# Adaptive norm, two Mamba passes and a gated FFN: products of u by B of five units moved from GpSimd to TensorE, as products with diagonal matrices

## What is computed

```python
h = layernorm(x) * (1 + ca) + sa
yf = sigmoid(mamba(h, forward weights));  yb = sigmoid(mamba(h reversed, backward weights))
x = x + ga * (layernorm(0.5 * (yf + yb reversed)) * ln_g + ln_b + h)
x = x + gb * ffn(layernorm(x) * (1 + cb) + sb)          # 256 -> 1024 -> 1024 -> 1024 -> 256
# mamba, 512 inner channels, 16 states per channel:
xi = silu(conv4(h @ in_proj));  z = h @ in_proj2
dt, B, C = split(xi @ x_proj, [64, 16, 16]);  dt = softplus(dt @ dt_w + dt_b)
u = dt * xi
for each channel d, state s, token t:   hs[t] = exp(dt[t] * A[d, s]) * hs[t-1] + u[t] * B[t, s]
y[t] = sum over s of hs[t] * C[t, s] + D * xi[t];   out = (y * silu(z)) @ out_proj
```

## Time and profile before

| | us |
|---|---|
| median of 3 runs (lowest, highest) | 4833.41 (4833.06, 4835.86) |
| the profiled execution, its own time | 4838.41 |
| its span, first to last instruction | 4836.5 |
| PE busy | 4305.1 (89%) |
| DVE busy | 3992.5 (83%) |
| POOL busy | 3464.0 (72%), nearly all before 3480 us |
| ACT busy | 3250.3 (67%) |
| granted TensorE clock, mean of the core | 0.965 |

### The profile page before, as it was taken

The page is one execution under the profiler, slowest core; times in us unless marked ns, Lnnn a source line. Parts: engine busy times, 40 slices in busy tenths (PEclk is TensorE's granted clock), DMA queues, the critical chain, the costliest instruction groups (busy, mean ns, idle before and its releaser), DMA issues. The chain is left out here.

```text
span 4836.5 us, 61589 instructions
## 1 busy us (share of the span) xinstructions
PE 4305.1 (89%) x22500; PEld 3149.4 (65%) x22500; DVE 3992.5 (83%) x4222; ACT 3250.3 (67%) x5217; POOL 3464.0 (72%) x1623
## 2 busy tenths in 40 slices
PE   7888888888888888888888888888799999999999
PEld 3565556556555656665555556555678888888888
DVE  6999999999999999999999999999944444444452
ACT  7777777777777777777777777777444444444443
POOL 5999999999999999999999999999820000000000
PEclk9999999999999999999999999999899999999999
DMA  7433333333333333333333333333230111010100
GB/s 264 140 122 124 114 119 114 107 122 112 127 114 116 116 109 118 117 114 118 111 114 111 110 113 114 112 115 127 93 126 31 35 31 36 31 36 31 35 22 9
DMA packets 176850, 475.34 MB, mean 98 GB/s; under 512 B 15073, under 2 KB 99809, under 8 KB 141921
## 3 DMA queue, kind: packets, MB, share of 16 engines
q1 hardware_dynamic: 175648, 459.83, 28.1%
q10 hardware_dynamic: 896, 11.54, 0.7%
HBM read 435.66 MB, written 47.19 MB: 100 GB/s over the span
## 5 line engine op out<-in xcount | busy, mean ns | idle before, releaser
L1293 DVE TENSOR_TENSOR_SCAN m_h<-bank,m_state,m_dBx 128x512 f32<-128x512 f32 x1792 | 2182.1, 1263 | 35.3 <-ACT bank L1059 29.1
L794 PEld LDWEIGHTS bank<-ident,m_h 128*128 128x128 f32 x8192 | 1009.0, 147 | 655.4 <-issue 335.7
L794 PE MATMUL bank<-ident,m_h 128*128 128x128 f32 x8192 | 1244.5, 283 | 163.0 <-DVE m_h L1302 103.5
L1183 POOL TENSOR_TENSOR m_dBx<-u,m_Bs 128x1024 f32<-128x1024 f32 x512 | 1199.8, 2371 | 2.2 <-issue 0.2
L1183 POOL TENSOR_TENSOR m_dBx<-m_u,m_Bs 128x1024 f32<-128x1024 f32 x512 | 1199.1, 2370 | 2.7 <-DVE m_h L1293 0.6
L1302 DVE TENSOR_TENSOR m_h<-m_h,bank 128x1024 f32<-128x1024 f32 x736 | 880.6, 1197 | 26.0 <-PE bank L776 22.8
L1059 ACT ACTIVATE bank<-m_dt,cols 128x512 f32<-128x512 f32 x1024 | 691.1, 688 | 237.9 <-DVE m_h L1293 234.8
L1059 ACT ACTIVATE bank<-dt,cols 128x512 f32<-128x512 f32 x1024 | 690.7, 688 | 214.7 <-DVE m_h L1293 211.3
L776 PEld LDWEIGHTS bank<-ident,m_Ct 128*128 128x128 f32 x2944 | 345.7, 143 | 678.5 <-DVE m_h L1302 461.4
L776 PE MATMUL bank<-ident,m_Ct 128*128 128x128 f32 x2944 | 486.2, 290 | 315.8 <-DVE m_h L1302 313.1
L296 POOL TENSOR_TENSOR mvj<-mvj,norm_c 128x4 f32<-128x4 f32 x16 | 16.2, 1015 | 984.5 <-DVE mvj L257 984.5
(11 more groups left out here) (165 smaller groups left out, 5206.6 us busy)
## 6 DMA issues: line engine op xcount, KB each, us to landing
m_Bs<-b_dram SPq DMA_DIRECT2D x256, 1024.0 KB, 4.8
m_Cs<-c_dram SPq DMA_DIRECT2D x288, 256.0 KB, 3.2
xx<-in_x SPq DMA_DIRECT2D x16, 512.0 KB, 7.1
xn_dram<-xx SPq DMA_DIRECT2D x16, 512.0 KB, 4.4
yb_dram<-m_ysb SPq DMA_DIRECT2D x16, 512.0 KB, 6.8
xx<-xn_dram SPq DMA_DIRECT2D x16, 512.0 KB, 3.8
x_dram<-m_ysb SPq DMA_DIRECT2D x16, 512.0 KB, 6.8
base<-xn_dram SPq DMA_DIRECT2D x16, 512.0 KB, 3.9
```

The source lines that it names most:

```text
L794: mm = pe.matmul(YB[b][:, o:o + P], h[:, k % NH, m, tok:tok + P], ident[:, :], start=(s == 0 and o == 0), stop=False, is_transpose=True, s ...
L1183: pool.tensor_tensor(dBx[:, k % NDBX, :, :], u[ch.batch][:, m, :], Bs[:, k // BP % 2, k % BP, :].unsqueeze(1).broadcast_to((P, 2, T)), ALU ...
L1293: dve.tensor_tensor_scan(h[:, k % NH, m, flip(ch)], DA[ch.at(STEPS, i) % NDA][:, flip(ch)], dBx[:, k % NDBX, m, flip(ch)], initial, ALU.mu ...
```

## The change

Five units, A_UNITS = 19, 22, 25, 28, 31, get their products u * B from PE. For each, SP loads a matrix with B of 512 tokens as four 128x128 diagonal blocks (dg, 256 KB, two buffers), and PE multiplies the transposed u of the half (uT, made once per chunk by eight transposes and two copies of ACT) by it into the DA bank of the step, at the step two before the scan (fill_a). The decays of these units go to the unit's h buffer in SBUF, and the scan reads them there and the products from the bank, and writes over the decays. The diagonals get to DRAM by four strided stores of single numbers per chunk, into zeroed memory, seen as rows of 513 numbers so that a column is a diagonal of the 512-wide matrix (store_diagonals); SP issues them behind the loads of the chunk, ahead of the next chunk's first loads of B. In turn the product by C of three more units goes to POOL (P_UNITS from nine to twelve). Some jobs move: output products from steps 29 and 35 to 32 and 38, the last two z products from 54 and 56 to 56 and 57, and on SP the store of the next chunk's B and C behind load_b(6). In the prologue ten stores of 256 KB zero the diagonal matrices, and the loads of ln_g, ln_b and w3_s move to the last chunk; the tile of ones goes.

```diff
 J_Y, J_OUT, J_C = (19, 20, 21, 22), (23, 24), 25
-AT = {J_LN: (0, 1), J_X: (3, 5, 7, 9), J_CONV: (11, 16, 20, 24), J_DT: (35, 40, 43, 49), J_Z: (50, 52, 54, 56),
-      J_Y: (46, 47, 13, 17), J_OUT: (29, 35)}
-AT_LN, AT_X, AT_CONV, AT_DT, AT_Z, AT_Y, AT_OUT = (AT[j] for j in (J_LN, J_X, J_CONV, J_DT, J_Z, J_Y, J_OUT))
+J_UT = (26, 27)
+AT = {J_LN: (0, 1), J_X: (3, 5, 7, 9), J_CONV: (11, 16, 20, 24), J_DT: (35, 40, 43, 49), J_Z: (50, 52, 56, 57),
+      J_Y: (46, 47, 13, 17), J_OUT: (32, 38), J_UT: (26, 29)}
...
-P_UNITS = (1, 5, 7, 9, 13, 15, 17, 21, 25)
+P_UNITS = (1, 5, 7, 9, 13, 15, 17, 18, 20, 21, 24, 26)
+A_FIRST, A_STEP, NA = 19, 3, 5
+A_UNITS = tuple(A_FIRST + A_STEP * i for i in range(NA))
+B_UNITS = tuple(k for k in range(NU) if k not in A_UNITS)
+NBU, NDG, DIAG = len(B_UNITS), 2, T + 1
...
+            def store_diagonals(ch):
+
+                wait_drained(sp, ch, J_B)
+                if ch.first():
+                    sp.sem_inc(S["go"], 1)
+                    sp.wait_ge(S["d_init"], 16 * BATCH * NA)
+                s = B0 + A_FIRST - DS
+                by_diagonal = d_dram[ch.batch].rearrange("i (p w) -> i p w", w=DIAG)
+                for n in range(TS):
+                    sp.dma_start(by_diagonal[:, :, n * P], dbB[s:s + A_STEP * (NA - 1) + 1:A_STEP, n * P:(n + 1) * P],
+                                 allow_slow_non_contiguous=True).then_inc(S["d_st"], 16)
+
...
+            def load_d(ch, i):
+
+                n = ch.at(NA, i)
+                wait(sp, S["a_fill"], 2 * (n - NDG + 1))
+                if i == 0:
+                    sp.sem_inc(S["go"], 1)
+                    sp.wait_ge(S["d_st"], ch.at(64, 64))
+                sp.dma_start(dg[:, n % NDG, :, :], d_dram[ch.batch, i, 0:P * T].rearrange("(p t c) -> p t c", t=TS, c=P)
+                             ).then_inc(d_in[n % NDG], 16)
...
+                load_b(ch, 6)
                 if has(ch, 1):
                     store_b(ch.go(1))
-                load_b(ch, 6)
+                load_d(ch, 2)
                 load_c(ch, 8)
+                load_c(ch, 9)
+                load_d(ch, 3)
                 load_b(ch, 7)
+                load_c(ch, 10)
                 if has(ch, -1):
                     store_y(ch.go(-1))
+                load_c(ch, 11)
+                load_d(ch, 4)
                 if has(ch, 1):
+                    store_diagonals(ch.go(1))
                     load_b(ch.go(1), 0)
                     load_b(ch.go(1), 1)
...
+            def fill_a(ch, g):
+
+                for i, k in enumerate(A_UNITS):
+                    m = g - (2 * k - 2)
+                    if not 0 <= m < 2:
+                        continue
+                    n, tile = ch.at(NA, i), ch.at(STEPS, 2 * k + m)
+                    if m == 0:
+                        if i == 0:
+                            wait_drained(pe, ch, J_UT[1])
+                        pe.wait_ge(d_in[n % NDG], 16 * (n // NDG) + 16)
+                    pe.wait_ge(S["scan"], tile - NDA + 1)
+                    for s in range(TS):
+                        mm = pe.matmul(DA[tile % NDA][:, s * P:(s + 1) * P], uT[:, s, m * P:(m + 1) * P],
+                                       dg[:, n % NDG, s, :], start=True, stop=True)
+                    mm.then_inc(S["a_fill"], 1)
 
...
+                            turn_u(ch, g, m)
+                        fill_a(ch, g)
                         if has(ch, 1):
...
-                wait(act, S["scan"], ch.at(STEPS, k - NDA + 1))
+                if j in A_UNITS:
+
+                    if m == 0:
+                        act.wait_ge(S["turned"], ch.at(NU, j - NH + 1))
+                    out = h[:, j % NH, m, :]
+                else:
+                    wait(act, S["scan"], ch.at(STEPS, k - NDA + 1))
+                    out = DA[ch.at(STEPS, k) % NDA][:, :]
                 m += 2 * half
...
+            def keep_uT(ch, k):
+                for m in range(2):
+                    if k == AT_UT[m] + ACT_LAG:
+                        wait_filled(act, ch, J_UT[m])
+                        wait(act, S["a_fill"], ch.at(2 * NA, 0))
+                        b = BANK[J_UT[m]]
+                        act.copy(uT[:, :, m * P:(m + 1) * P], FB[b][:, :].rearrange("p (t n) -> p t n", n=P)
+                                 ).then_inc(drain[b], 1)
 
...
-                                       initial, ALU.mult, ALU.add).then_inc(S["scan"], 1)
+                o, da = h[:, k % NH, m, flip(ch)], DA[ch.at(STEPS, i) % NDA][:, flip(ch)]
+                if k in A_UNITS:
+                    dve.wait_ge(S["a_fill"], ch.at(2 * NA, 2 * A_UNITS.index(k) + m + 1))
+                    decays, share = o, da
+                else:
+                    decays, share = da, dBx[:, dbx_ring(ch, k) % NDBX, m, flip(ch)]
+                dve.tensor_tensor_scan(o, decays, share, initial, ALU.mult, ALU.add).then_inc(S["scan"], 1)
 
```

More of the change, by code:

```diff
@@ L470, in weighed, with made, dbx_ring @@
             return sum(j < k for j in (P_UNITS if k in P_UNITS else D_UNITS))
+        def made(k):
+            return sum(j < k for j in B_UNITS) if k >= 0 else sum(j < k + NU for j in B_UNITS) - NBU
+        def dbx_ring(ch, k):
+            return ch.at(NBU, made(k))
         pieces = []
@@ L542, in store_b @@
                 sp.dma_start(c_dram[ch.batch], dbB[B0 + DS:B0 + 2 * DS, :]).then_inc(S["b_st"], 16)
+            def store_diagonals(ch):
[8 more added lines that the diff above has]
+                                 allow_slow_non_contiguous=True).then_inc(S["d_st"], 16)
             def load_b(ch, j):
-                wait(sp, S["dbx"], ch.at(NU, BP * (j - 1)))
+                wait(sp, S["dbx"], ch.at(NBU, made(BP * (j - 1))))
                 if j == 0:
@@ L592, in prologue @@
                 sp.dma_start(fcol[:, :, :], a["ffn_cols"]).then_inc(S["lng_in"], 16)
-                for i, name in enumerate(("ln_g", "ln_b", "w3_s")):
-                    sp.dma_start(lng[:, i, :], a[name].partition_broadcast(P)).then_inc(S["lng_in"], 16)
+                sp.wait_ge(S["d_zero"], 1)
+                for b in range(BATCH):
+                    for i in range(NA):
+                        sp.dma_start(d_dram[b, i, 0:P * T].rearrange("(p t c) -> p t c", t=TS, c=P), dg[:, 0, :, :]
+                                     ).then_inc(S["d_init"], 16)
                 for n in range(6, 10):
@@ L599, in prologue @@
                 store_b(ch)
+                store_diagonals(ch)
                 for j in range(2):
@@ L616, in load_ffn @@
                         sp.dma_start(wm(k, j), a["wmod"][k * P:(k + 1) * P, j * T:(j + 1) * T]).then_inc(S["wm2_in"], 16)
+                for i, name in enumerate(("ln_g", "ln_b", "w3_s")):
+                    sp.dma_start(lng[:, i, :], a[name].partition_broadcast(P)).then_inc(S["lng_in"], 16)
                 J.load_base(sp, (0, 0), xn_v, x_v)
@@ L633, in body @@
                 load_c(ch, 1)
+                load_d(ch, 0)
+                load_d(ch, 1)
                 if has(ch, 2):
@@ L743, in turn_y, with turn_u @@
                     turn(J_Y[m], lambda s: acc[:, s, o:o + P], ch)
+            def turn_u(ch, g, m):
+                if g == AT_UT[m]:
+                    if m == 0:
+                        pe.wait_ge(S["u_ready"], ch.at(2, 2))
+                    turn(J_UT[m], lambda s: u[ch.batch][:, 2 + m, s * P:(s + 1) * P], ch)
+            def fill_a(ch, g):
[13 more added lines that the diff above has]
+                    mm.then_inc(S["a_fill"], 1)
             def tail(ch, g):
@@ L953, in front @@
                     wait(act, S["b_st"], ch.at(32, 0))
+                    if not ch.first():
+                        act.sem_inc(S["go"], 1)
+                        act.wait_ge(S["d_st"], ch.at(64, 0))
                     rows = B0 + 2 * DS
@@ L1171, in weigh_b @@
             def weigh_b(ch, k):
+                if k not in B_UNITS:
+                    return
                 half, s = divmod(k, DS)
                 m = slice(2 * half, 2 * half + 2)
-                if k % BP == 0:
+                if k == next(i for i in B_UNITS if i // BP == k // BP):
                     j = k // BP
@@ L1181, in weigh_b @@
                     pool.wait_ge(S["p_ne"], 2 * NPIECE)
-                wait(pool, S["scan"], ch.at(STEPS, 2 * (k - NDBX) + 2))
-                pool.tensor_tensor(dBx[:, k % NDBX, :, :], u[ch.batch][:, m, :],
+                held = unit(ch, B_UNITS[made(k) - NDBX] - (NU if made(k) < NDBX else 0))
+                if held:
+                    pool.wait_ge(S["scan"], held[0].at(STEPS, 2 * held[1] + 2))
+                pool.tensor_tensor(dBx[:, dbx_ring(ch, k) % NDBX, :, :], u[ch.batch][:, m, :],
                                    Bs[:, k // BP % 2, k % BP, :].unsqueeze(1).broadcast_to((P, 2, T)),
@@ L1345, in prologue @@
                             for b in range(BATCH):
-                                last = dve.tensor_scalar(cbc[:, k, b, :], ones[:, :], cs[:, k, b:b + 1], None, ALU.mult)
```

(1 more changed line is left out.)

41 lines of the change are left out of this document (23 added, 18 removed).

## The result

| | before | after |
|---|---|---|
| median, us (lowest, highest; 4 runs each) | 4834.64 (4833.06, 4836.36) | 4886.20 (4885.89, 4887.08) |
| the profiled execution, us (its span) | 4838.41 (4836.5) | 4887.08 (4885.3) |
| granted TensorE clock | 0.965 | 0.984 |
| first scan / last scan, us from the start | 72.61 / 3480.21 | 72.37 / 3531.32 |

The ratio is 1.0103 (95% interval 1.0091 to 1.0116): the changed kernel is 1% slower, where 0.6% faster was forecast. The loss stands between the first and the last scan, a stretch that is 51.35 us longer; the prologue is 0.24 us shorter, and the part behind the last scan 2.3 us shorter, which is no more than the executions of one kernel differ by (4833.06 to 4836.36). In the first 31 chunks it is (3352.66 - 3304.69) / 31 = +1.55 us each, and the last chunk has 3.4 more.

A forecast was written before the change was run, and what follows sets the result against it. DVE was taken as the bound, 104.2 us of work per chunk, with POOL also full. Per chunk -0.9 x 31 = -29, last chunk -3, prologue +2 gave -30: 4808 profiled, 4803 median, range 4745 to 4860.

The forecast's parts named there:

- three signs of being wrong: Step 44's wait under 1 us, PE's tiles of 60 and 61 at double times, or L1183 idling behind DMA m_Bs.
- DVE's products, -3.3: DVE loses three products by C of 1.11 us per chunk, 3.3 us less work.
- Waits at steps 37 to 39, +0.6; at 44 and 45, +3.2: New DVE waits behind PE per chunk: 0.6 us at steps 36 to 39, 3.1 at step 44, 0.1 for scan 45.
- The waits of steps 44, 45 and 53, -0.85: DVE's old waits behind PE at steps 45 and 53, 0.47 and 0.38 us, are covered or go.
- Placement of the scans, 0; tiles 0.88: Scans reading decays from SBUF and products from a bank cost nothing extra; one PE tile of four products takes 0.88 us.
- rival 2: PE's lower clock at the chunk's turn doubles tiles of steps 60 and 61: +1.7 us per chunk, 4856; chance 0.17.
- The wait of step 63, -0.56: ACT makes unit 31's decays before its table loads, so DVE's 0.56 us wait in step 63 goes.
- The last chunk, -3: The last chunk, without front work of a next one, keeps its 3 us gain.
- The prologue, +2: In the prologue ten 256 KB stores replace three 128 KB loads: +2 us (0 to 8).
- Rival 1, PE keeps pace: No PE tile is late: -4.7 us per chunk, 4686, or 4750 with half of step 42's wait; chance 0.18.
- Rival 3, slow stores: Slow diagonal stores delay the loads of B behind them; at 25 us POOL starves DVE, 5080; chance 0.12.
- POOL, 4 to 5 us idle: POOL, losing five products and gaining three, should show 4 to 5 us of idle per chunk.

The follow-up runs named there:

- experiment 2: Changed kernel with the last two groups of z's matmuls and copies put back from steps 56 and 57 to 54 and 56: 4870.74 us.
- experiment 3: Changed kernel with unit 26's product by C given back from POOL to DVE and its load of C removed: 4886.45 us.
- experiment 11: Changed kernel with diagonal units 23, 25, 27, 29, 31, their loads moved and ACT's silu of z one step later: 4885.84 us.

## Why the prediction was wrong

Forecast 4803, measured 4886.2, outside the range (4745 to 4860). Two steps failed: what DVE waits for at step 63, and the waits that the removed products had covered. None of the three signs of being wrong that the prediction named came up; only its distance of 105.1 us from chunk to chunk, which is 107.4, showed it. Its terms per chunk, against the means of the table:

- **DVE's products, -3.3.** DVE's work (chunk less idle time) fell from 103.77 to 100.77, 3.0. Near; a scan behind a wait can't start inside the record of the one before it, about 0.08 us each time (1.26 long, 1.18 apart), and DVE waits 6.4 times a chunk where it waited 4.0. That makes 0.2 of the 0.3.
- **Waits at steps 37 to 39, +0.6; at 44 and 45, +3.2.** Measured 0.47 more, and 3.15 + 0.03 in all. The walk through PE's order step by step, with durations from the earlier trace rows, met the wait at step 44 within 0.05 us, and its stages too: ACT takes dt 1.00 us after step 42 (2527.33; forecast 1.08), and the tile is there after 5.4 (2531.77; forecast 5.5). That is the mechanism, and not luck.
- **The waits of steps 44, 45 and 53, -0.85.** They went, 0.94 in the mean.
- **Placement of the scans, 0; tiles 0.88.** Both right. The tile of step 60 goes from 2557.78 to 2558.67, 0.89 us at full speed, where rival 2 wanted 1.76. The stretch at a lower granted clock is still there (0.83 in the 10 us from 2562, as in the earlier trace rows), but the tiles are made before it: it stands behind PE's pause of 3.61 us that ends at 2565.09 (granted 1.00 from 2561.5 to 2565, 0.51 from 2565 to 2568.5).
- **The wait of step 63, -0.56: this step failed.** "ACT can make those of unit 31 (steps 62, 63) before its table loads" was read from what the decay waits for, its buffer, and not from its place in ACT's order: z_silu stands at step 62 between the two decays of that unit. Freed of the buffer, the decay of step 62 came early; that of 63 could not. And two parts of the change made DVE arrive there earlier or ACT later, which the sum had at nothing: z's last copies moved by a step or two (experiment 2, 0.82 us), and the product of unit 26, which had stood in front of this wait (experiment 3, 1.14 us). +1.33 for -0.56, 1.9 us a chunk, 59 us in 31: three quarters of the miss of 79 (4887.1 for 4808, both of the profiled execution). That the silu stands there was to be read from the kernel before. ACT goes to its table load right behind the decay of step 62 and makes that of step 63 after the second load:

```profile
2204.64 0.69 ACT L1059 ACTIVATE bank<-m_dt,cols 128x512 f32<-128x512 f32 x1 [0.48 <-DVE m_h L1293]
...
2205.35 1.28 ACT L1008 ACT_TABLE_LOAD   x1
2206.64 1.06 ACT L1008 ACTIVATE m_z<-m_z 128x1024 f32<-128x1024 f32 x1
...
2209.10 0.69 ACT L1059 ACTIVATE bank<-m_dt,cols 128x512 f32<-128x512 f32 x1
```

- **Step 47, nothing in the sum: failed by the same rule.** The product of unit 18 stood between the wait of step 44 and this one; without it DVE comes 1.1 us earlier, to a decay behind dt's copies. +0.52, 16 us in all. That products lay there as a cover was to be read from DVE's order, and with PE's lag from the prediction's own walk.
- **The last chunk, -3.** It has 3.4 us more. DVE waits 7.4 us in it for 1.3, most of it for PE's tiles and spreads of C (5.4 at steps 37 to 45, 2.0 at steps 56, 57 and 63), and PE has rows of the FFN part to do there; without unit 22 it is back at 102.8 us, as before (102.9).
- **The prologue, +2.** -0.2.
- **The sum.** 0.3 + 1.9 + 0.5, less 0.2 for the terms that came out smaller, is the 2.5 us between -0.9 and +1.55 a chunk. The prediction's own -0.91 x 31 is -28, where it has -29; that moves the forecast by 1 us.
- **Rival 1, PE keeps pace:** no. **Rival 3, slow stores:** not in the changed kernel. In its issue table m_Bs lands in 5.2 us (4.8 before), and POOL waits for B 1.3 us in all, with 101888 packets under 512 bytes where there were 15073:

```profile
DMA packets 297737, 545.77 MB, mean 112 GB/s; under 512 B 101888, under 2 KB 186624, under 8 KB 262784
```

The last write of a chunk's four stores begins 8.3 to 9.6 us after the first is issued (13 chunks of pass 2), and the prediction took 8. The stores do have a price on SP, 5.4 us of issue for four, which experiment 11 shows as soon as B is short of time behind them. The Trainium skill (DMA: Bandwidth & Descriptors, "Rules for kernel authors") warns of one descriptor per element; the packets agree, 86815 more of them under 512 bytes, and no run here shows them to harm other transfers beyond the landing times, 5.2 us for 4.8 (m_Bs) and 3.5 for 3.2 (m_Cs).

- **POOL, 4 to 5 us idle.** 7.4, since DVE is slower than forecast and POOL waits for it through the saved states.

The chance given to slower, 0.23, lay all in the clock and the stores. The mechanism that decided, waits uncovered and a decay behind a silu, was in none of the rivals.

The Trainium skill (ScalarE: Activation LUTs, "What ACT_TABLE_LOAD costs") gives 1283 ns for a load and 1380 more for a drain. The trace shows 1.28 us for the load and the next activation 1.30 after its start (2558.13 to 2559.43), so without the drain; the pair around the silu holds ACT for 2.6 us beside the silu's 1.06. An estimate from the page's two figures for a pair would be 5.3, which the trace does not bear out.

## What to carry to other kernels

Work taken from an engine that waits is worth only what doesn't stand in front of a wait: list the engine's waits first, and for each the work between it and the one before. When a wait on a buffer goes, look at what stands ahead of the instruction in its own engine's order. And where an in-order engine lags most, ask nothing new of it: leaving out the one late tile of five (with its load put right), and one number in ScalarE's order, turned 1% slower into 1% faster.
